# Box sums of two pooling levels on accumulating transfers, and the group norm's sums earlier in the step

## The reference

```python
x = x + conv_block(group_norm(x))
x = x + attention(group_norm(x))       # 1024 tokens, softmax over 1024
```

```python
y1.append(0.9 * maxpool(y1[-1]) + 0.1 * sumpool(y1[-1]) / 25)      # chain 1
y2.append(sumpool(e * y2[-1]) / (sumpool(e) + 1e-6))               # chain 2
y = concat(silu(cv1(concat(y1))), silu(cv2(concat(y2))))           # 512 channels
a = c1(ddwv(ddwh(dwv(dwh(y)))))                                    # depthwise taps, then 1x1
return silu(cvend(y * a))
```

## Time and profile before

| | us |
|---|---|
| median of 3 runs | 1458.1 (1456.68 to 1458.79) |
| time of the profiled execution | 1458.25 |
| its span, first to last instruction | 1456.5 |
| mean granted clock of TensorE | 0.952 of full speed |
| TensorE busy | 1292.0 (89%) |
| VectorE busy | 1143.7 (79%) |
| ScalarE busy | 691.9 (48%) |
| GpSimd busy | 128.8 (9%) |
| bytes moved by transfers | 62.84 MB |

### The profile page before, as it was taken

How to read it: one execution, slowest core, us unless ns; L and a number is a source line. 1 busy time by engine, 2 the same in 40 slices (tenths; PEclk the granted TensorE clock), 3 DMA queues, 4 the chain that set the end, 5 groups by cost and what they waited for, 6 DMA issues and landing times.

```text
span 1456.5 us, 18340 instructions
## 1 busy us (share of the span) xinstructions
PE 1292.0 (89%) x7162; PEld 1077.5 (74%) x7162; DVE 1143.7 (79%) x1218; ACT 691.9 (48%) x749; POOL 128.8 (9%) x64
## 2 busy tenths in 40 slices
PE   3649898872999999999999999999999999999797
PEld 1238797742768986888688878877986798688597
DVE  7858686678689887988798798879877998796443
ACT  0335564562246536543654365347435653564333
POOL 1645363200000000000000000000000000000000
PEclk9778998985999999999999999999999999999899
DMA  7401122210000020001002000200020002000000
GB/s 286 158 15 73 58 93 82 88 58 0 29 15 1 16 87 14 0 33 68 14 0 72 29 14 0 72 29 14 0 94 6 14 14 86 0 1 30 29 1 29
DMA packets 19175, 62.84 MB, mean 43 GB/s; under 512 B 1600, under 2 KB 4288, under 8 KB 19136
## 3 DMA queue, kind: packets, MB, share of 16 engines
q1 hardware_dynamic: 18432, 62.00, 11.4%
q10 hardware_dynamic: 704, 0.30, 0.1%
HBM read 36.61 MB, written 25.17 MB: 42 GB/s over the span
## 4 chain that ended last, share of the span: by engine, by line
PE 63%; issue 14%; DVE 12%; ACT 5%; DMA 0%; DVEq 0%; ACTq 0%; POOLq 0%; POOL 0%
PE slot L1094 21%; PE slot L1132 12%; PE ps_o L1132 9%; PE ps_ey L565 6%; DVE between L1407 4%; PE slot L549 3%; PE slot L1148 3%; PE ps_e L549 3%; DVE a L1407 2%; PE slot L1072 2%; PE ps_t L633 1%; PE slot L1119 1%; PE ps_ot L1164 1%; ACT f_all L1283 1%; PE slot L1055 1%
## 5 line engine op out<-in xcount | busy, mean ns | idle before, releaser
L1132 PE MATMUL slot<-f_all,q_all 128*128 128x512 f32 x768 | 196.9, 409 | 13.4 <-ACT pooled L1273 13.4
L1132 PE MATMUL ps_o<-v_all,pt_all 128*128 128x256 f32 x1536 | 199.2, 286 | 5.4 <-ACT mixed L1292 5.2
L1132 PEld LDWEIGHTS ps_o<-v_all,pt_all 128*128 128x128 f32 x1536 | 188.8, 192 | 7.6 <-DVE pt_all L1411 6.2
L1132 PEld LDWEIGHTS slot<-f_all,q_all 128*128 128x128 f32 x768 | 145.2, 195 | 43.9 <-ACT pooled L1273 14.8
L1407 DVE SCALAR_TENSOR_TENSOR a<-between,k_columns,a 128x992 f32<-128x992 f32 (+1 forms) x128 | 157.5, 1232 | 4.9 <-ACT a L1264 2.6
L1287 ACT CAST v_all<-y 128x1024 fp32r<-128x1024 f32 x32 | 33.7, 1052 | 185.8 <-DVE y L1438 185.8
L1411 DVE TENSOR_TENSOR pt_all<-slot,pt_all 128x1024 fp32r<-128x1024 f32 x64 | 78.2, 1222 | 47.5 <-ACT pt_all L1278 47.5
L1072 PE MATMUL slot<-wide,k_cv 128*128 128x512 f32 x256 | 114.3, 597 | 0.0
L565 PE MATMUL ps_ey<-box,x_all 128*128 128x192 f32 (+2 forms) x480 | 95.5, 358 | 19.6 <-DVE rmc L751 12.8
L565 PEld LDWEIGHTS ps_ey<-box,x_all 128*128 128x128 f32 x480 | 84.2, 204 | 26.3 <-issue 20.2
L1264 ACT ACTIVATE a<-between,k_columns 128x1024 f32<-128x1024 f32 x64 | 79.5, 1242 | 48.7 <-DVE between L1407 47.7
(11 more groups left out here) (160 smaller groups left out, 2649.3 us busy)
## 6 DMA issues: line engine op xcount, KB each, us to landing
levels<-x_all SPq DMA_DIRECT2D x32, 512.0 KB, 2.6
x_all<-in_x SPq DMA_DIRECT2D x8, 1024.0 KB, 13.2
q_all<-levels SPq DMA_DIRECT2D x8, 1024.0 KB, 4.9
x<-in_x SPq DMA_DIRECT2D x8, 1024.0 KB, 4.8
out<-x SPq DMA_DIRECT2D x8, 1024.0 KB, 3.9
pooled<-levels SPq DMA_DIRECT2D x8, 512.0 KB, 3.3
wide<-levels SPq DMA_DIRECT2D x7, 512.0 KB, 3.3
x_all<-in_w_c SPq DMA_DIRECT2D x2, 512.0 KB, 3.6
```

Of the source, the lines that this page charges most:

```text
L1132: last = nc.tensor.matmul(out, lhs, rhs, start=(n == 0), stop=(n == len(parts) - 1))
```

## The change

Levels 1 and 2 of chain 1 get their box sums, in the middle steps, from accumulating transfers that GpSimd issues. The levels stand in `middle`, in rows of 34 elements with two zeros at the end of each (`PITCH`), so that a shifted copy of the whole level is one transfer of 128 x 1088 fp32 (544 KB). ScalarE copies the level to `row_sums` (`begin_rows`), four transfers in turn add it shifted by 1, -1, 2, -2; ScalarE copies the result to `box_sums` (`begin_columns`), and four more add it shifted by rows. Each transfer waits for the one before. Level 0 stays on TensorE, but is turned from a buffer of its own, `first_level`, into `ps_level`, which is `ps_o` and `ps_ot` taken together, between `cv2(1)` and `cv1(0)`, and is summed between `cv1(0)` and `cv1(1)`. `means` goes between `cv2(0)` and `cv2(1)`, `variances` behind `cv2(1)`. VectorE makes the maxima of level 0 at the start of the step, around the norm's small operations. Step 0 keeps TensorE for all its levels, through ScalarE copies into `first_level`.

```diff
+SHIFTS = (1, -1, 2, -2)
-TURN_AT, BOX_AT = 1, TILES - 2
+ROWS_AT, COLUMNS_AT, SECOND_AT = 0, 2, 6
+    def begin_rows(self, act, i, level):
+        wait(act, self.done, i, MIX * level)
+        self.nc.scalar.copy(self.row_sums[:, 0:ROWS], self.middle[:, level - 1, 2:2 + ROWS]).then_inc(self.rows_begun.sem, 1)
+    def begin_columns(self, act, i, level):
+        wait(act, self.rows_added, i, 4 * 16 * level)
+        self.nc.scalar.copy(self.box_sums[:, 0:ROWS], self.row_sums[:, 0:ROWS]).then_inc(self.columns_begun.sem, 1)
+    def add_rows(self, pool, i, level):
+        for n, d in enumerate(SHIFTS):
+            if n:
+                wait(pool, self.rows_added, i, 16 * (4 * (level - 1) + n))
+            else:
+                wait(pool, self.rows_begun, i, level)
+            pool.dma_start(self.row_sums[:, 0:ROWS], self.middle[:, level - 1, 2 + d:2 + d + ROWS],
+                           accum_op=ALU.add).then_inc(self.rows_added.sem, 16)
+    def mixture_of_added(self, dve, i, level):
+        wait(dve, self.columns_added, i, 4 * 16 * level)
...
@@ sync
+                    sp.dma_start(first_level[:, :], levels[i + 1]).then_inc(chain.first_in.sem, 16)
@@ gpsimd, behind the pow
+                if chained and attn:
+                    for level in range(1, LEVELS):
+                        chain.add_rows(pool, i + 1, level)
+                        chain.add_columns(pool, i + 1, level)
@@ slot_uses
-                    uses += [("zt", 0)] * (chained and t == TURN_AT) + [("zb", 0)] * (chained and t == BOX_AT)
@@ tensor
                 if conv:
                     cv2(0)
+                if attn:
+                    means()
+                if conv:
                     cv2(1)
-                    wait(pe, chain.loaded, i, 16)
-                    cv1(0, between=means if attn else None)
                 if attn:
                     variances()
+                if chained and attn:
+                    wait(pe, norm, i - 1, 6)
+                    turn_level(0)
                 if conv:
+                    wait(pe, chain.loaded, i, 16)
+                    cv1(0)
+                    if chained and attn:
+                        box_level(0)
                     cv1(1)
...
-                        if chained and t == TURN_AT:
-                            turn_level(0)
-                        if chained and t == BOX_AT:
-                            box_level(0)
...
-                            if chained:
-                                turn_level(1)
-                        if chained and m == (2 if attn else KT - 1):
+                        if chained and not attn and m == KT - 1:
                             box_level(1)
...
-                        if chained and m == 0:
+                        if chained and not attn and m == 0:
                             turn_level(2)
-                        if chained and m == 1:
+                        if chained and not attn and m == 1:
                             box_level(2)
@@ scalar
+                        if chained and t == 0:
+                            level_hi(0)
...
                     centre_tap(BEFORE - 2)
+                    if chained:
+                        chain.begin_rows(act, i + 1, 1)
...
                         exponent(t)
+                        if chained and t == COLUMNS_AT:
+                            chain.begin_columns(act, i + 1, 1)
+                        if chained and t == SECOND_AT:
+                            chain.begin_rows(act, i + 1, 2)
...
                     gated_hi(0)
+                    gated_hi(1)
                     if chained and attn:
-                        level_hi(1)
-                    gated_hi(1)
+                        chain.begin_columns(act, i + 1, 2)
@@ vector
+                if chained and attn:
+                    level_maxima(0, 0, 1, 2, 3)
                 if attn:
                     small = Steps(dve, norm, i - 1)
...
+                if chained and attn:
+                    level_maxima(0, 4, 5, 6)
                 if attn:
                     wait(dve, group_var, i - 1, 1)
...
                         if attn and n == BEFORE - 3:
+                            if chained:
+                                level_mixture(0)
                             break
...
+                            if chained:
+                                level_maxima(1, 0, 1)
...
+                        if chained and t < 5:
+                            level_maxima(1, t + 2)
+                        if chained and t == SECOND_AT:
+                            level_mixture(1)
+                            level_maxima(2, 0, 1)
+                        if chained and t > SECOND_AT:
+                            level_maxima(2, 2)
...
-                    level_maxima(1, 3, 4)
+                    if attn:
+                        level_maxima(2, 3, 4)
...
                         nc.vector.bn_aggr(mv[:, m, :], stats[:, m].rearrange("p h s -> p (h s)")).then_inc(bn.sem, 1)
+                if chained and attn:
+                    level_mixture(2)
```

More of the change, by code:

```diff
@@ L190, in sum_rows, with maxima @@
         return self.sum_a[:, :].rearrange("p (h w) -> p h w", w=W)
-    def maxima(self, dve, i, level, *steps):
-        src, pairs, tall = self.inner(level), self.pairs, self.tall
+    def maxima(self, dve, i, level, *steps, source=None):
+        early = level == 0 and source is not None
+        src, pairs, tall = source if early else self.inner(level), self.pairs, self.tall
         m4, four = image2d(self.work_b[:, :]), image2d(self.work_a[:, 0:N])
@@ L199, in maxima @@
             if step == 0:
-                wait(dve, self.loaded, i, 16)
+                if early:
+                    wait(dve, self.first_in, i - 1, 16)
+                else:
+                    wait(dve, self.loaded, i, 16)
                 self.larger(own, pairs[:, :, 2:W + 1], src[:, :, 0:W - 1], src[:, :, 1:W], first=True)
@@ L236, in mixture_of_sums @@
         self.mixture(dve, 0, level, self.sum_b[:, :, :])
-    def mixture_of_boxes(self, dve, i, level, slot):
-        wait(dve, self.boxed, i, level + 1)
-        self.mixture(dve, i + 1, level, image2d(slot))
 class Pooled:
@@ L1070, in cv1 @@
                                 wait(pe, chain.done, i, MIX * k)
-                            rows = chain.wide[:, k, h * HALF:(h + 1) * HALF]
-                            last = nc.tensor.matmul(slot[:, h * HALF:(h + 1) * HALF], keep["cv1"][:, k, cols(m)], rows,
+                            rows = chain.inner(k)[:, h * (H // 2):(h + 1) * (H // 2)]
+                            last = nc.tensor.matmul(image2d(slot[:, h * HALF:(h + 1) * HALF]), keep["cv1"][:, k, cols(m)], rows,
                                                     start=(k == 0), stop=(k == KT - 1))
@@ L1153, in mix @@
                     wait(pe, qv_lo, i - 1, 4)
+                    if t == 0 and chained:
+                        wait(pe, chain.done, i + 1, MIX)
                     if t:
@@ L1295, in level_hi @@
                 def level_hi(level):
-                    chain.turned_hi(act, i, level, slots_of["zt", level][:, :], zt_hi[:, :])
+                    slot = ps_level if attn else slots_of["zt", level]
+                    chain.turned_hi(act, i, level - (0 if attn else LEVELS - 1), slot[:, :], zt_hi)
                 if conv and not attn:
@@ L1371, in step @@
                     gated_hi(3)
+                    if chained and not attn:
+                        chain.copy_level(act, 2)
                 if chained:
@@ L1482, in step @@
                     outer_taps(next(before))
+                if chained and attn:
+                    outer_taps(next(before))
+                    level_lo(0)
                 if attn:
@@ L1546, in step @@
                     add_attention(TILES - 1)
[L1547 to L1548 removed]
                 if chained:
[L1550 removed]
+                    if attn:
+                        level_maxima(2, 3, 4)
+                    else:
+                        level_maxima(1, 3, 4)
                 if conv:
```

158 lines of the change are left out of this document (96 added, 62 removed).

## The result

The changed kernel takes 1504.85 us (median of 5 runs, 1504.7 to 1506.59) against 1458.67 of the kernel before on the same chip (1456.68 to 1459.97): a ratio of 1.0321 with a 95% interval of 1.0307 to 1.0336. It is slower by 3.2%, 46 us; the prediction was 1498, a ratio of 1.027.

A forecast was written before the change was run, and what follows sets the result against it. TensorE's own list was taken to bound the kernel; per middle step -6.3 + 7.0 + 5.2, taken as 6.3 us, six steps 37.8 and 1.8 more: 1458.25 + 39.6 = 1497.9 us. Range 1445 to 1565.

The forecast's parts named there:

- What goes from TensorE: Middle step: turn and box matmuls of levels 1 and 2 leave TensorE, -6.3 us; level 0's 3.14 us only move.
- The start of the step: From `cv2(0)`: TensorE waits 1.7 us at `means`, 4.8 at `turn_level(0)`, loses 1.85 to the clock; balance +7.0 a step.
- The tile loop: Wins at tiles 1 and 2; at tile 6 `begin_rows(2)` waits for `mixture(1)`, delaying `turn(7)`; balance of waits +5.2 us.
- The transfers: Sixteen accumulating transfers a step, taken at 5.5 us each, 22 for four, hidden within windows of 25.6 to 30 us.
- The two passes: Each accumulating transfer taken as two passes, 5.5 us, between 2.6 (one pass) and 8.3 (three in turn).
- the rival with 1527 to 1589 us: Transfers come late: 1527 us in all at 7 us each, 1589 at 8.3; chance 0.28.
- The cover of 6.4 us a transfer: All four transfer windows of a step hold up to 6.4 us per transfer before anything shows.
- the last window: Column transfers of level 2, up to `mixture(2)`: a window of 25.6 us for four transfers.
- The rival on the other side: The norm comes in time, `turn_level(0)` does not wait, 8.35 us fall off: -2.1 a step, 1446 us; chance 0.14.
- the floor of 1420: Lowest time if the norm comes in time and tile 6 costs less too: six times 6.3 us saved.

The follow-up runs named there:

- the kernel with 1152: The changed kernel with `PADDED` = 1152, not 1092, so later buffers lie 1024 bytes further on than in the kernel before: 1503.39 us, ratio 1.0312.
- the first experiment: The changed kernel with all seven maxima of level 0 moved behind the second normalised half and the taps: 1509.16 us, ratio 1.0356.
- the best version: The changed kernel with level 0's last three maxima behind the norm, mixture(1) at tile 5, level 2's last two maxima in idle time, rows of 1152: 1451.49 us.
- the three mended together: The changed kernel with maxima 4 to 6 of level 0 behind the norm, mixture(1) one tile earlier and rows of 1096: 1466.09 us, ratio 1.0022.

## Why the prediction was right

The direction, the size and the places were right; the sum was 39.6 us, the result 46. The terms of a middle step add up to 5.9 us, and the prediction took 6.3 with only rounding as the reason; a middle step took 7.0 more.

- **What goes from TensorE**, -6.3: measured -5.5 from `c1(0)` to `cv2(0)`. The matmuls went; the 144 products around them became slower, by 144 x 0.0066 = 0.95 us. The prediction had considered the rows' stride in `cv1` as a cost and taken it at nothing, and never that a longer buffer moves all others. The stride was rightly taken at nothing: in the change four products of `level_middle`, whose rows are 34 elements apart, take 1.72 us from start to start (730.91 to 732.63), as four of `level_ends`, whose rows touch, do (732.63 to 734.35). Most of the 0.95 does not show in the length of a middle step: with the pace of before, the same time goes to the means and to a longer stretch at the lower clock, as the kernel with 1152 shows.
- **The start of the step**, from `cv2(0)` on: +10.1 predicted, +10.0 measured. `turn_level(0)` starts 17.8 us behind `cv2(0)` (846.48 to 864.28), the predicted 50.9 - 33.1 = 17.8. Its wait is 4.57 (4.8 predicted), the means' 1.06 (1.7 predicted; 1.54 where the pace is that of before), the clock fell as supposed. Moving three maxima took away the wait and 3.35 us of the step, which shows the cause. That all seven could go was my own mistake in the first experiment: I had followed the norm's chain and not the chain from the mixture of level 0 through ScalarE's copy to the queries.
- **The tile loop**: +2.1 predicted, +2.7 measured, by the mechanism named. Half of the difference is a reading: the 62.0 us of before come from the chain's row of `c1(0)` (644.62); by the timelines, which the measured rows use, it is 61.7 and the forecast +2.4. `begin_rows(2)` waited 4.83 us (4 to 5 predicted), and the mixture one tile earlier took away 3.2 of the step. TensorE's two waits were 2.92 and 1.57, in sum 4.5, where some 5 at `turn(7)` were written. What the prediction did not see is that `box_level(0)` had filled the time in which ScalarE works ahead of `turn(7)`: "Level 0's 3.14 us only move" holds for the matmuls and not for the time. In the change ScalarE is late there anyway, so the sum did not suffer; it is the repairs that could not win back these 1.8 us.
- **The transfers**: taken at 5.5 us each, measured 4.5 to 4.7 to landing and 5.2 from issue to issue (751.44 to 756.68). The two passes were a choice between the bounds 2.6 and 8.3, so that coming this near was in part luck. The windows held, as the kernel without transfers shows, and the rival with 1527 to 1589 us is excluded. The Trainium skill's figures, as the prediction combined them (DMA: Bandwidth & Descriptors, Anatomy of one DMA, with two sources read as in Collectives: The Full Stack, The bandwidth ceiling), gave an estimate of 4.6, and these rows agree with it. The cover of 6.4 us a transfer was too rosy for the last window: one transfer took 7.4 us from issue to issue there (838.86 to 846.27 in the profile after), behind two loads that SP had issued at 835.61 and 836.85, and what was left there was 2.4 us in all, not 3.6 (25.6 less the 22 of four at 5.5).
- **The rest**: the first `score(0)` of the loop came 12.5 us later than before (443.05 to 455.51), 11.6 predicted; the five steps to 1188.45 took 7.0 more each, 6.3 predicted; from there to the end it is 0.8 us more, where the prediction had 3.5 less. That last difference, 4.3 us, is half of what is missing. Some 2 us of it is step 6, whose tile loop took 60.15 us before and not 61.7, so that it had less to win; 0.8 lies between `c1(0)` and `cv2(0)` of that step, where the slower products are. Another 1.55 is the tile loop of step 7, which makes no chain: 58.54 us against 56.99. In both kernels TensorE waits 1.99 us there ahead of `turn(7)`; before, its eight transposes then took 1.09 us, after 1.66 (granted clock 1.00 in the 1.8 us behind the wait before, 0.59 in the 2.0 us after). The other runs show loops of 58.5 and of 57.0 us, also with the edits of one list alone (57.0 with the mixture one tile earlier), so no run ties this part to the change.
- **The rival on the other side**, the norm in time and 1446 us, was not what the change does, but its mechanism is real: with three maxima behind the norm, two in idle time, the mixture at tile 5 and the buffers at a multiple of 1024 bytes the same change gives 1451.5. Its price was too high. It counted the wait for the norm and the clock at 4.8 + 1.85 = 6.65 us a step, and getting the norm early was worth 3.35. And the floor of 1420 counts no wait at all, where 1.39 us at `turn_level(0)` and 1.8 at `turn(7)` are left in every middle step of the best version.

Not settled: what in the address makes a product take 0.2333, 0.2283 or 0.2267 us; three places of the buffers were tried beside that of before, and which operand counts was not. Open is too what decides whether the clock falls behind a wait of 1.8 to 2.0 us.

## What to carry to other kernels

Work taken from the engine that bounds the kernel is worth something only if the two others still deliver in time: write down for each engine the list from its last input to the operation that the bound engine waits for, and put work that nobody waits for behind it or into idle time, here five small maxima, and one mixture a tile earlier: with these alone the ratio went from 1.0321 to 1.0001, 47 us. And when work moves away, ask what time it had filled: the 2.27 us of level 0's sum left a wait of 1.8 behind them. Follow every list in which a moved operation's result is awaited, ScalarE's too: the first repair moved the stall by 30 us and won nothing. And when a change alters the size of a buffer, compare the duration of untouched instructions, and test it in the version that the engine bounds: in the other one most of the cost is hidden.

## What the runs showed of the hardware

- A 512-column matmul of the convolutions, with the same instruction and clock, takes 0.2267, 0.2283 or 0.2333 us by where the buffers lie (1024, 576 or 544 bytes behind those of the kernel before, which has 0.2267). Where TensorE bounds the kernel the difference from first to last is 0.5% of the time.
- An accumulating transfer of 544 KB within the on-chip memory lands 4.7 us after its issue on GpSimd, and in a chain each takes 5.2 us; shortly behind 1024 and 512 KB loads of the other queue one took 7.4. 52 MB of them a run slowed neither the products nor the other engines measurably.
- Behind waits of 1.39 us TensorE's eight transposes took 1.09 us, full speed, in all middle steps but one (1.58, with another wait of 1.08 us shortly ahead). Behind 1.81 to 1.83 us they took 1.09 to 1.20 in 16 of the 18 steps of the last three kernels with transfers (the three mended together, and the two with the maxima in idle time), but 1.37 to 1.46 in five of six with the mixture one tile earlier alone. Behind the same 1.99 us they took 1.09 before the change and 1.66 after. Behind 4.57, and behind 2.92 followed by 1.3 to 1.6, they took 1.97, the lower level of 1.2 GHz, in every middle step of the change.
